# Cross-attention and gated feed-forward on one core: gather and splits ahead of masks and exponentials in step 7

## Chip, cores, metric

The kernel runs on one core of one Trainium2 chip. The metric is the device time of one execution in microseconds (us); lower is better. Engines are named as in the profile: PE is TensorE (PEld its weight loads), DVE is VectorE, ACT is ScalarE, POOL is GpSimd, SP is SyncE, which issues all transfers.

## What is computed

One transformer layer: cross-attention of 16 sequences of 128 tokens on 16 contexts of 128, then a gated feed-forward part, both with a residual. Cut to what matters:

```
x = x + xattn(layernorm(x), ctx)      # 32 heads of width 32, 8 groups of keys and values
x = x + (silu(h1) * h2) @ w3.T + b3   # h1, h2 = layernorm(x) @ w12.T + b12
# xattn: scores = q @ k.T / sqrt(32), masked; softmax; @ v; @ w_out.T
```

All arrays are float32. The kernel makes every product from pairs of float16: a value is split in a high and a low part, and a product is three matrix products (high by high, high by low, low by high).

## The kernel before, in words

The tokens come in 8 blocks of 256 (two sequences, `AB`). The attention part is a software pipeline of iterations t = 1 to 8, each of 8 steps s = 0 to 7. Iteration t does the attention of block t - 1, one group of 4 heads for 2 sequences per step (unit number g = 8 (t - 1) + s), and beside it the projections of block t (q in 8 units, k in 2, v in 2) and the output projection of block t - 2. The feed-forward part follows and is not touched here.

Each engine has its own instruction list, written out by hand in the same pair of loops, and waits on semaphores. What an engine does in a step is fixed; when, depends on the waits.

In step 7 (`LAST`) of iterations 2 to 6 the work is, by engine:

- **PE** (L1407 to L1485): the scores of group g (`scores`, L1464); the turning of one column, the largest absolute values of the next context block (`turn_top`, L1393, one row of 128 into a PSUM bank); the first half of v (`v_proj`, L1407); the turning of the first x tile of the block after next's projections, in two halves (`turn_x`, L1416, 4 + 4 instructions); the weighing of v with the probabilities of group g - 3 (`weigh`, L1485); the turning of the second x tile; the second half of v; and `spread_top` (L1400). Then step 0 of the next iteration: scores (L1464) and the first q unit (L1407), which begins only when all low parts of both x tiles have been written (`pe.wait_ge(s_dread, done("x", 2 * t + 1, 1))`).
- **DVE**: `mask_scores(g)` (L1889), eight instructions that scale and mask the scores and take each row's extreme; `gather_top` (L1687 to L1698), five small instructions that turn the gathered column into a power of two, the first of which frees its bank; `norm_prob(g, 0)` (L1905, L1908), which hands the inverse sums of the first sequence to POOL; the low part of v (`v_lo`, L1859) and of the first x tile (`x_lo`, L1854, two); the low part of the attention output of g - 3 (`attn_lo`, L1929); `norm_prob(g, 1)` (L1905, L1911); the two low parts of the second x tile; the low part of v's second half; `take_top` (L1710).
- **ACT**: `exps(g, 0)` (L1203, four exponentials with their sums), which waits for the first half of the masks; high part of v (L1193) and of the first x tile (L1166, two); high part of the attention output (L1173); `exps(g, 1)`; high parts of the second tile and of v's second half; high part of the probabilities (`prob_hi`, L1218).
- **POOL**: the low part of the probabilities of g - 1 (L975, two), and the normalising of the first sequence (L981).

A high part must be written by ACT before DVE takes the low part from the same PSUM bank; the low part frees the bank. Five banks go round (`banks()`), and the least recently taken is next. So in step 7 the first half of the second x tile goes into the bank of the gathered column, the second half into that of v, the second half of v into that of the first half of the first tile.

In iterations 3 to 6 DVE also looks at the weights of the feed-forward part for their maxima: in steps 2, 4 and 6 it reads 128 x 2048 values that SP has loaded into `look` (`max_of`, L1725; the load is L762). In step 6 this stands at the end of the step, behind `norm_prob(g, 1)` and `q_lo` (L1859). Iteration 6 has two more small instructions behind it, `in_pairs` (L1731, L1732), which join the maxima two by two.

Of the kernel before, what the change touches and what calls it, by code (L numbers as in the profile page):

```python
# [41 lines left out]
NB = TOK // AB  # L42
# [39 lines left out]
LAST = 7  # L82
# [68 lines left out]
def first_unit(t, s):  # L151

    if t < NB and s in FIRST_Q:
        return "q", t, FIRST_Q[s]
    if t >= 2 and s in FIRST_O:
        return "o", t - 2, FIRST_O[s]
    if t < NB and s == LAST:
        return "v", t, 0
    return projection(t, s) if t == 1 else None
# [8 lines left out]
def x_tiles(t, s):  # L168

    if t < NB - 1 and s == LAST:  # L170
        return 2 * t + 2, 2 * t + 3
    if t == NB - 1 and s in (3, LAST):
        return (2 * NB, 2 * NB + 1) if s == 3 else (2 * NB + 2, 2 * NB + 3)
    return None, None
# [133 lines left out]
def by_pool(g):  # L308

    return g in NORMED and g % GROUPS >= 3 and g < 56  # L310


def normed_count(g, kind=lambda n: n in NORMED):
# [33 lines left out]
def xattn_ffn(nc, x, ctx_t, mask, wq_t, wk_t, wv_t, wo_t, w12_t, b12_t, w3_t, b3_row, out):  # L347
# [8 lines left out]
    with ExitStack() as stack:  # L356
# [719 lines left out]
        def _(act):  # L1076
# [120 lines left out]
            def exps(g, u):  # L1197
                act.wait_ge(s_neg, U * g + u + 1)
                for j in range(HPG):
                    h = HPG * u + j  # L1200
                    head = e[:, g % 2, u, SEQ * j:SEQ * j + SEQ]
                    if g in NORMED:
                        ins = act.activation(head, head, ACT.Exp, bias=neg_max[:, g % 2, h:h + 1], scale=-1.0,  # L1203
                                             accum_out=p_sum[:, g % 2, u, j:j + 1])
                    else:
                        ins = act.activation(head, head, ACT.Exp, bias=neg_max[:, g % 2, h:h + 1], scale=-1.0)  # L1206
                ins.then_inc(s_exp, 1)
# [89 lines left out]
            def unit_hi(key):  # L1297
                if key and key[0] == "q":
                    q_hi(*key[1:])
                elif key and key[0] == "k":  # L1300
                    k_hi(*key[1:])
                elif key and key[0] == "v":
                    v_hi(*key[1:])

            for t in range(1, NB + 1):
                for s in range(STEPS):
                    g, (tile, tile2) = GROUPS * (t - 1) + s, x_tiles(t, s)
                    exps(g, 0)
                    if t == NB and s - 1 in H_AT:
                        hid_hi(0, H_AT[s - 1])  # L1310
                    if t == NB and s in H_AT:
                        exps(g, 1)
                        prob_hi(g)
                        silus(0, H_AT[s])
                        attn_hi(g - 3)
                        continue
                    unit_hi(first_unit(t, s))
                    if tile is not None:
                        x_hi(tile, 0)
                        x_hi(tile, 1)  # L1320
                    if g >= 3:
                        attn_hi(g - 3)
                    exps(g, 1)
                    if tile2 is not None:
                        x_hi(tile2, 0)
                        x_hi(tile2, 1)
                    unit_hi(second_unit(t, s))
                    if t < NB - 1 and s in (4, 6):
                        scale_rows(2 * t + s // 2)
                    prob_hi(g)  # L1330
                    if t == NB - 1 and s in (2, 6):
                        scale_rows(2 * NB + (s - 2) // 2)
                        scale_rows(2 * NB + (s - 2) // 2 + 1)
                    if t == 1 and s == 2:
                        o_high()
# [336 lines left out]
        def _(dve):  # L1672
# [396 lines left out]
            for t in range(1, NB + 1):  # L2069
                a = t - 1  # L2070
                block_scales(a)
                if t == 2:
                    link(dve.tensor_scalar(out_base[:, :], w_es[:, 0, col("o")], w_es[:, 0, col("kv", 1)], C_OUT,
                                           ALU.mult, ALU.mult))
                if t >= 2:
                    output_scales(t - 2)
                for s in range(STEPS):
                    g, name, (tile, tile2) = GROUPS * a + s, top_at(t, s), x_tiles(t, s)
                    if g >= 3:
                        divide(g - 3)  # L2080
                    mask_scores(g)
                    if t == NB and s - 1 in H_AT:
                        hid_lo(0, H_AT[s - 1])
                    if name:
                        gather_top(name)
                    if g >= 1 and g - 1 not in PLO_AWAY:
                        prob_lo(g - 1)
                    if g in NORMED:
                        norm_prob(g, 0)
                    if g in NORMED and t == NB and s in H_AT:  # L2090
                        norm_prob(g, 1)
                    unit_lo(first_unit(t, s))
                    if tile is not None:
                        x_lo(tile, 0)
                        x_lo(tile, 1)
                    if t == NB and s in H_AT:
                        first_half_read(0, H_AT[s])
                    if g >= 3:
                        attn_lo(g - 3)
                    if t < NB - 1 and s == 5:  # L2100
                        max_of(f"ctx{t + 1}", ctx_next, s_ctxload, 16 * t + 32)
                    if t == NB - 2 and s == 3:
                        max_of("b12", b12[:, :], s_b12, 16)
                    if (t, s) in O_LOW_AT:
                        o_low(O_LOW_AT.index((t, s)))
                    if t < NB - 1 and s in (2, 3):
                        row_stats(2 * t + s)
                    if t == NB - 1 and s in (1, 5):
                        row_stats(2 * NB + (s - 1) // 2)
                        row_stats(2 * NB + (s - 1) // 2 + 1)  # L2110
                    if t == NB - 1 and s == 4:
                        ffn_factors()
                    if g in NORMED and not (t == NB and s in H_AT):
                        norm_prob(g, 1)
                    if tile2 is not None:
                        x_lo(tile2, 0)
                        x_lo(tile2, 1)
                    unit_lo(second_unit(t, s))
                    if look_at(t, s):
                        max_of(look_at(t, s), look, s_look, look_count(look_at(t, s)))  # L2120
                    if look_at(t, s) == "w7":
                        in_pairs()
                    if t == NB and s in H_AT:
                        gate(0, H_AT[s])
                    if name:
                        take_top(name)
# [119 lines left out]
```

## Time and profile before

| | us |
|---|---|
| median of 3 runs (lowest to highest) | 1042.55 (1042.33 to 1042.89) |
| the profiled execution | 1045.69 |
| its span, first to last instruction | 1043.9 |
| PE busy | 1013.3 (97%) |
| DVE busy | 701.5 (67%) |
| ACT busy | 480.7 (46%) |
| POOL busy | 524.4 (50%) |

The span is shorter than the execution by what lies before the first and after the last instruction. Busy time says how long an engine had an instruction in hand; the ends of matrix products are modelled. A group that is called "DVE small L1687" is an instruction of DVE that writes the tile `small` on line 1687.

### The profile page before, as it was taken

What the parts mean: (1) busy time and instruction counts of PE and PEld (TensorE: products, weight loads), DVE (VectorE), ACT (ScalarE), POOL (GpSimd) and SP (SyncE); (2) the same over time, 40 slices, a digit from 0 to 9 for tenths busy, and PEclk for the clock granted to TensorE, in tenths of its full rate; (3) what the DMA queues carried; (4) which work ended last, traced back from release to release, by engine and by line L of the source; (5) the groups of instructions that cost most, each with busy time, mean ns of one, the idle gap of its engine ahead of it and who ended that gap; (6) DMA issues with size and microseconds to landing.
All of it is one profiled execution on the core that took longest, in us unless ns stands there. A gap on an engine that the chain in (4) does not pass through costs nothing.

```text
span 1043.9 us, 22125 instructions
## 1 busy us (share of the span) xinstructions
PE 1013.3 (97%) x8312; PEld 674.2 (65%) x8312; DVE 701.5 (67%) x2168; ACT 480.7 (46%) x1335; POOL 524.4 (50%) x500
## 2 busy tenths in 40 slices
PE   8897999999999999899999999999999999999998
PEld 7776867767677676676644444444444888468853
DVE  6789988878888788878769333746864446625431
ACT  5767666767666675664767310123431112211110
POOL 2869923746547375289967697148742301212000
PEclk8999999999999999999999999999999999999999
DMA  9559796998999989789854726494759641974301
GB/s 364 221 155 203 156 227 155 220 254 223 241 222 213 261 211 249 190 203 264 211 155 111 230 89 218 76 345 166 273 197 194 231 113 42 218 246 122 82 31 51
DMA packets 230779, 199.13 MB, mean 191 GB/s; under 512 B 177040, under 2 KB 187280, under 8 KB 225808
## 3 DMA queue, kind: packets, MB, share of 16 engines
q1 hardware_dynamic: 230672, 197.72, 70.5%
q8 instruction: 66, 1.08, 0.4%
q14 instruction: 41, 0.34, 0.1%
HBM read 119.04 MB, written 35.65 MB: 148 GB/s over the span
## 4 chain that ended last, share of the span: by engine, by line
PE 82%; DVE 8%; ACT 2%; issue 1%; DMA 1%; SPq 0%; DVEq 0%; ACTq 0%
PE bank_dense L1407 51%; PE bank_spare L1407 12%; PE bank_score L1563 6%; PE bank_spare L1563 6%; PE bank_av L1563 3%; DVE arena_attn L1889 3%; PE bank_score L1464 2%; DVE arena_in L1725 1%; PE bank_dense L1485 1%; DVE arena_attn L1899 1%; DMA k_scratch<-arena_in 1%; PE bank_spare L1485 1%; ACT arena_attn L1203 1%; PE bank_spare L1416 0%; ACT L1229 0%
## 5 line engine op out<-in xcount | busy, mean ns | idle before, releaser
L1407 PE MATMUL bank_dense<-arena_rows,arena_in 128*128 128x256 f16 (+1 forms) x1272 | 177.8, 298 | 1.6 <-POOL arena_in L913 1.0
L1407 PE MATMUL bank_dense<-arena_attn,arena_rows 128*128 128x512 f16 x768 | 166.4, 379 | 0.0
L975 POOL TENSOR_TENSOR arena_attn<-arena_attn 128x512 f16<-128x512 f32 x89 | 101.9, 1162 | 118.1 <-ACT arena_attn L1218 118.1
L1203 ACT ACTIVATE arena_attn<-arena_attn,arena_in 128x128 f32<-128x128 f32 x352 | 136.4, 391 | 47.8 <-DVE arena_in L1889 47.6
L1407 PEld LDWEIGHTS bank_dense<-arena_rows,arena_in 128*128 128x128 f16 x1272 | 123.0, 99 | 46.1 <-DVE arena_in L1737 1.3
L1889 DVE CUSTOM_DVE_ANT_0 arena_attn<-bank_score,arena_in 128x128 f32<-128x128 f32 x512 | 143.7, 346 | 1.6 <-PE bank_score L1464 1.1
L1407 PEld LDWEIGHTS bank_dense<-arena_attn,arena_rows 128*128 128x128 f16 x768 | 75.1, 98 | 90.2
L1407 PE MATMUL bank_dense<-arena_out,arena_attn 128*128 128x512 f16 x576 | 127.8, 379 | 0.0
L1407 PEld LDWEIGHTS bank_dense<-arena_out,arena_attn 128*128 128x128 f16 x576 | 55.5, 98 | 63.4
L1407 PE MATMUL bank_spare<-arena_rows,arena_in 128*128 128x256 f16 (+1 forms) x648 | 87.7, 293 | 0.0
L1407 PE MATMUL bank_dense<-arena_out,arena_in 128*128 128x512 f16 x384 | 83.0, 379 | 0.0
L1218 ACT ACTIVATE arena_attn<-arena_attn 128x1024 f16<-128x1024 f32 x64 | 67.3, 1052 | 27.9 <-DVE arena_attn L1911 27.7
L913 POOL TENSOR_TENSOR arena_in<-arena_in 128x512 f16<-128x512 f32 x62 | 75.5, 1217 | 5.0
L1995 DVE SCALAR_TENSOR_TENSOR arena_out<-bank_dense,small,arena_out 128x256 f32<-128x256 f32 x64 | 28.0, 478 | 74.1 <-PE bank_dense L1407 74.1
L1407 PEld LDWEIGHTS bank_spare<-arena_rows,arena_in 128*128 128x128 f16 x648 | 62.2, 98 | 19.9
L1407 PEld LDWEIGHTS bank_dense<-arena_out,arena_in 128*128 128x128 f16 x384 | 37.5, 98 | 45.4
L1203 ACT ACTIVATION_READ_ACCUMULATOR arena_attn<-arena_attn,arena_in 128x1 f32 x352 | 66.7, 189 | 0.0
L1206 ACT ACTIVATE arena_attn<-arena_attn,arena_in 128x128 f32<-128x128 f32 x160 | 50.9, 392 | 33.2 <-DVE arena_in L1889 33.2
L923 POOL TENSOR_TENSOR small<-small 128x1 f32<-128x1 f32 x32 | 20.3, 637 | 88.4 <-DVE small L1778 88.3
L1407 PE MATMUL bank_dense<-arena_in 128*128 128x256 f16 x456 | 54.0, 276 | 1.4 <-DVE arena_in L1744 1.4
L1051 POOL TENSOR_TENSOR arena_out<-arena_out,arena_rows 128x1024 f32<-128x1024 f32 x12 | 29.2, 2462 | 46.6 <-DMA arena_out<-x_scratch 46.6
L1407 PEld LDWEIGHTS bank_dense<-arena_in 128*128 128x128 f16 x456 | 44.2, 99 | 8.9 <-DVE arena_in L1744 1.7
(238 smaller groups left out, 1888.1 us busy)
## 6 DMA issues: line engine op xcount, KB each, us to landing
arena_rows<-x SPq DMA_DIRECT2D x32, 512.0 KB, 5.8
arena_in<-w_scratch SPq DMA_DIRECT2D x64, 256.0 KB, 3.0
arena_attn<-q_scratch SPq DMA_DIRECT2D x48, 256.0 KB, 4.4
arena_rows<-w_t SPq DMA_DIRECT2D x12, 1024.0 KB, 6.6
arena_rows<-ctx_t SPq DMA_DIRECT2D x8, 1024.0 KB, 6.0
q_scratch<-arena_attn SPq DMA_DIRECT2D x16, 512.0 KB, 5.2
x_scratch<-arena_rows SPq DMA_DIRECT2D x16, 512.0 KB, 3.9
arena_out<-x_scratch SPq DMA_DIRECT2D x16, 512.0 KB, 5.9
```

What stands on the lines that cost most here:

```text
L913: pool.tensor_tensor(lo, buf, hi, ALU.subtract).then_inc(ready, 1)
L975: ins = pool.tensor_tensor(p_split[:, g % 2, u, 1], e[:, g % 2, u], p_split[:, g % 2, u, 0], ALU.subtract)
L1051: ins = pool.tensor_tensor(y_res[:, u], y_res[:, u], b3_all, ALU.add)
L1203: ins = act.activation(head, head, ACT.Exp, bias=neg_max[:, g % 2, h:h + 1], scale=-1.0, accum_out=p_sum[:, g % 2, u, j:j + 1])
L1206: ins = act.activation(head, head, ACT.Exp, bias=neg_max[:, g % 2, h:h + 1], scale=-1.0)
L1218: act.activation(p_split[:, g % 2, :, 0], e[:, g % 2], ACT.Copy).then_inc(s_phi, 1)
L1407: ins = pe.matmul(dst, lhs(a, c), rhs(b, c), start=(c == chunks[0] and n == 0), stop=(c == chunks[-1] and n == 2))
L1464: ins = pe.matmul(B_SCORE[:, HALF * u + SEQ * j:HALF * u + SEQ * j + SEQ], q_stack[0:3 * DH, m // 4, j, m % 4, SEQ * u:SEQ * u + SEQ], k_s ...
L1485: ins = pe.matmul(dst[DH * j:DH * j + DH, SEQ * u:SEQ * u + SEQ], v[:, a % 2, u, m, 0:DH], prob_t[:, g % 2, u, piece, j], start=n == 0, st ...
L1563: ins = pe.matmul(seven(v, j), weights[:, a, P * c:P * c + P], rows[:, b, c], start=(c == 0 and n == 0), stop=(c == 3 and n == 2))
L1889: ins = dve.tensor_tensor_reduce(out=e[:, g % 2, h // HPG, SEQ * (h % HPG):SEQ * (h % HPG) + SEQ], in0=B_SCORE[:, SEQ * h:SEQ * h + SEQ], ...
L1995: ins = dve.scalar_tensor_tensor(out=cols, in0=bank("y", f, q)[:, 256 * k:256 * k + 256], scalar=c_ffn[:, 2 * h + k:2 * h + k + 1], in1=co ...
```

## The change

In step 7 of iterations 2 to 6 (`unit_first`) DVE does gather, the low part of v's first half and the two low parts of the first x tile ahead of the masks, and ACT does the high parts of the same ahead of the first exponentials. The maximum of step 6 moves up on DVE, ahead of `norm_prob(g, 1)`; `in_pairs` moves from the end of step 6 of iteration 6 to behind the masks of step 7. No instruction is added or taken away, and the lists of PE, POOL and SP stay as they are.

```diff
+def unit_first(t, s):
+
+    return s == LAST and 2 <= t < NB - 1
...
+                    if unit_first(t, s):
+                        unit_hi(first_unit(t, s))
+                        x_hi(tile, 0)
+                        x_hi(tile, 1)
                     exps(g, 0)
...
-                    unit_hi(first_unit(t, s))
-                    if tile is not None:
+                    if not unit_first(t, s):
+                        unit_hi(first_unit(t, s))
+                    if tile is not None and not unit_first(t, s):
                         x_hi(tile, 0)
                         x_hi(tile, 1)
...
+                    if unit_first(t, s):
+                        gather_top(name)
+                        unit_lo(first_unit(t, s))
+                        x_lo(tile, 0)
+                        x_lo(tile, 1)
                     mask_scores(g)
+                    if t == NB - 2 and s == LAST:
+                        in_pairs()
                     if t == NB and s - 1 in H_AT:
                         hid_lo(0, H_AT[s - 1])
-                    if name:
+                    if name and not unit_first(t, s):
                         gather_top(name)
...
-                    unit_lo(first_unit(t, s))
-                    if tile is not None:
+                    if not unit_first(t, s):
+                        unit_lo(first_unit(t, s))
+                    if tile is not None and not unit_first(t, s):
                         x_lo(tile, 0)
                         x_lo(tile, 1)
...
+                    if look_at(t, s) and s == 6:
+                        max_of(look_at(t, s), look, s_look, look_count(look_at(t, s)))
                     if g in NORMED and not (t == NB and s in H_AT):
                         norm_prob(g, 1)
...
-                    if look_at(t, s):
+                    if look_at(t, s) and s < 6:
                         max_of(look_at(t, s), look, s_look, look_count(look_at(t, s)))
-                    if look_at(t, s) == "w7":
-                        in_pairs()
```

On ACT, steps 6 and 7 of iteration 5, before. `v_high` is the high part of v, arena_rows with a bank as its source the high part of an x tile, `x4` the four exponentials of one sequence, 128x256 from a bank the high part of q or of the attention output:

```order
L1180 ACTIVATE arena_attn<-bank_dense 128x256
L1218 ACTIVATE arena_attn<-arena_attn 128x2x512
L1203 ACTIVATE arena_attn<-arena_attn,arena_in 128x128 x4
L1193 ACTIVATE v_high<-bank_spare 128x8x32
L1166 ACTIVATE arena_rows<-bank_dense 128x4x128 x2
L1173 ACTIVATE arena_attn<-bank_dense 128x256
```

The same place of the changed kernel, whose lines are numbered 5 higher here:

```order
L1185 ACTIVATE arena_attn<-bank_dense 128x256
L1223 ACTIVATE arena_attn<-arena_attn 128x2x512
L1198 ACTIVATE v_high<-bank_spare 128x8x32
L1171 ACTIVATE arena_rows<-bank_dense 128x4x128 x2
L1208 ACTIVATE arena_attn<-arena_attn,arena_in 128x128 x4
L1178 ACTIVATE arena_attn<-bank_dense 128x256
```

The four exponentials have moved behind the high parts of v and of the first x tile.

On DVE, end of step 6 of iteration 5 and step 7, before. `ISA` with `bank_score` is a mask instruction, of which there are eight and one stands here; TENSOR_REDUCE of arena_rows is the weight maximum:

```order
L1929 SCALAR_TENSOR_TENSOR arena_attn<-bank_dense,arena_attn 128x256
L1911 SCALAR_TENSOR_TENSOR arena_attn<-arena_attn,bank_av 128x512
L1725 TENSOR_REDUCE arena_in<-arena_rows 128x1
L1889 ISA arena_attn,arena_in<-bank_score,arena_in 128x128
L1687 TENSOR_REDUCE small<-bank_spare 1x1
L1698 TENSOR_TENSOR small<-small 1x2
L1908 TENSOR_SCALAR arena_attn<-bank_av 128x4
L1859 SCALAR_TENSOR_TENSOR v_low<-bank_spare,v_high 128x256
L1854 TENSOR_TENSOR arena_rows<-bank_dense,arena_rows 128x4x128 x2
```

The same of the changed kernel, whose lines are numbered 10 higher here:

```order
L1939 SCALAR_TENSOR_TENSOR arena_attn<-bank_dense,arena_attn 128x256
L1735 TENSOR_REDUCE arena_in<-arena_rows 128x1
L1921 SCALAR_TENSOR_TENSOR arena_attn<-arena_attn,bank_av 128x512
L1697 TENSOR_REDUCE small<-bank_spare 1x1
L1708 TENSOR_TENSOR small<-small 1x2
L1869 SCALAR_TENSOR_TENSOR v_low<-bank_spare,v_high 128x256
L1864 TENSOR_TENSOR arena_rows<-bank_dense,arena_rows 128x4x128 x2
L1899 ISA arena_attn,arena_in<-bank_score,arena_in 128x128
L1918 TENSOR_SCALAR arena_attn<-bank_av 128x4
```

The masks have moved behind gather, v split and x splits, and the maximum ahead of the normalising of step 6.

## Rows read from the trace of the kernel before

**Rows 1.** Waits of PE, iterations 2 to 6: total us, times, longest.

```profile
PE bank_spare L1416 <- DVE small L1687: 3.2, 3, 1.1
PE bank_dense L1416 <- DVE small L1687: 2.9, 1, 2.9
PE bank_spare L1416 <- DVE v_low L1859: 2.3, 4, 0.6
PE bank_dense L1416 <- DVE v_low L1859: 0.6, 1, 0.6
```

**Rows 2.** Timeline, PE, step 7 of iteration 5: start, us, instruction, [idle].

```profile
363.62 2.78 PE L1407 MATMUL bank_spare<-arena_in 128*128 128x256 f16 x24
366.24 1.04 PE L1416 MATMUL bank_dense<-arena_in,arena_rows 128*128 128x128 f32 x8
...
370.66 2.79 PE L1407 MATMUL bank_dense<-arena_in 128*128 128x256 f16 x24
...
374.29 2.79 PE L1407 MATMUL bank_dense<-arena_rows,arena_in 128*128 128x256 f16 x24
```

**Rows 3.** Timeline, DVE, the same stretch.

```profile
364.02 2.28 DVE L1725 TENSOR_REDUCE arena_in<-arena_rows 128x1 f32<-128x2048 f32 x1
366.21 0.34 DVE L1889 CUSTOM_DVE_ANT_0 arena_attn<-bank_score,arena_in 128x128 f32<-128x128 f32 x1
...
369.92 1.28 DVE L1854 TENSOR_TENSOR arena_rows<-bank_dense,arena_rows 128x512 f16<-128x512 f32 x2
...
372.12 0.19 DVE L1905 RECIPROCAL bank_av<-arena_attn 128x4 f32<-128x4 f32 x1 [0.60 <-ACT arena_attn L1203]
...
372.95 1.28 DVE L1854 TENSOR_TENSOR arena_rows<-bank_spare,arena_rows 128x512 f16<-128x512 f32 x2
```

**Rows 4.** Timeline, ACT, the same stretch.

```profile
367.41 0.40 ACT L1203 ACTIVATE arena_attn<-arena_attn,arena_in 128x128 f32<-128x128 f32 x1 [1.69 <-DVE arena_in L1889]
...
368.97 0.36 ACT L1193 ACTIVATE v_high<-bank_spare 128x256 f16<-128x256 f32 x1
369.23 1.06 ACT L1166 ACTIVATE arena_rows<-bank_dense 128x512 f16<-128x512 f32 x2
370.18 0.38 ACT L1173 ACTIVATE arena_attn<-bank_dense 128x256 f16<-128x256 f32 x1
370.45 0.40 ACT L1203 ACTIVATE arena_attn<-arena_attn,arena_in 128x128 f32<-128x128 f32 x1
...
373.49 0.39 ACT L1193 ACTIVATE v_high<-bank_dense 128x256 f16<-128x256 f32 x1 [0.43 <-PE bank_dense L1407]
```

**Rows 5.** Timeline, PE, iteration 2: v's first half, next iteration's first projection.

```profile
170.81 2.78 PE L1407 MATMUL bank_spare<-arena_in 128*128 128x256 f16 x24
...
180.04 2.79 PE L1407 MATMUL bank_dense<-arena_rows,arena_in 128*128 128x256 f16 x24
```

**Rows 6.** Timeline, PE, the same two of iteration 6.

```profile
428.90 2.78 PE L1407 MATMUL bank_dense<-arena_in 128*128 128x256 f16 x24
...
442.77 2.78 PE L1407 MATMUL bank_dense<-arena_rows,arena_in 128*128 128x256 f16 x24
```

**Rows 7.** Timeline, DVE, the pairing of maxima in iteration 6.

```profile
431.60 0.64 DVE L1731 TENSOR_TENSOR arena_in<-arena_in 128x4 f32<-128x4 f32 x1
432.28 1.09 DVE L1732 COPY arena_in<-arena_in 128x4 f32<-128x4 f32 x1
```

**Rows 8.** Windows: stretch, us, PE busy (instructions), granted clock, DMA share, GB/s.

```profile
95.00:97.80 2.80, 0.00 (x0) 1.00 0.84 196
436.90:440.40 3.50, 3.27 (x16) 0.51 0.89 290
```

**Rows 9.** Timeline, POOL and DVE, iteration 2.

```profile
172.98 2.28 POOL L975 TENSOR_TENSOR arena_attn<-arena_attn 128x512 f16<-128x512 f32 x2 [4.95 <-ACT arena_attn L1218]
174.21 1.06 DVE L1698 TENSOR_TENSOR small<-small 1x2 f32<-1x2 f32 x1
```

**Rows 10.** Loads of `look` by SP (L762): us from issue to landing.

```profile
DMA to landing us min/median/max: 5.6/6.6/8.7
```

## The prediction

> **What bounds the kernel now.** The first view is the page: TensorE (PE) is busy 97% of the span, so only what keeps PE waiting, or slows it, can move the time. The second is the list of waits of PE over iterations 2 to 6 [rows 1]: all of its waits of any size there stand in front of line 1416, the turning of the next x tiles in step 7, 9.0 us together (3.2 + 2.9 + 2.3 + 0.6). Four times the releaser is the first instruction of the gather (small, L1687), which frees the PSUM bank that the gathered column stood in; five times it is the low split of v, which frees v's bank. By iteration that is 1.1 + 0.6 in 3, 4 and 5, 2.9 + 0.6 in 6, and for iteration 2 what is left of the v waits, 2.3 less three times 0.6, about 0.45.
>
> The third view is the timeline of one such step, iteration 5 [rows 2 to 4]. DVE takes the weight maximum (2.28), then the eight mask instructions from 366.21, then gather and v split, and the x splits from 369.92. PE had v ready at 366.4, stands 1.1 and 0.6 us on the way, and comes to v's second half at 370.66 only. The reader should look one step further, at what PE waits for next: the first projection of the next iteration, at 374.29, starts as soon as the low splits of the **second** x tile are done (two instructions from 372.95, 1.34 us before PE starts). In code: q of unit 0 waits for `done("x", 2t+1, 1)`. So in step 7 there are two chains that end at nearly one time: the banks, and masks, exponentials, normalising, splits of the second tile. The change shortens the first and lengthens the second.
>
> **The second chain, part by part** (iteration 5, all [rows 3, 4]). From the start M of the masks: first exponentials at M + 1.20 (366.21 to 367.41). They take 1.56 (v's high part starts at 368.97), v's and the first tile's high parts 1.21 (to 370.18), the attention copy 0.27, and the second exponentials start at 370.45, that is M + 4.24. Normalising comes 1.67 later (372.12), the second tile's low splits 0.83 later (372.95), PE's projection 1.34 later (374.29). Sum M + 8.08 today.
>
> *Exponentials.* The change takes v's and the first tile's high parts out from between the two exponential groups. That is 1.21 less; the attention copy stays. The chain behind the masks becomes M + 6.87.
>
> *Masks.* They now wait behind gather, v split and first-tile x splits. The gather no longer matters: its column is ready before v. What sets M is PE: v starts at V = 363.62, the eight turns end at 366.24 + 1.04 = 367.28, that is V + 3.66. An ACT operation starts 0.04 after PE's end (v's second half: PE ends 373.45, ACT starts 373.49) [rows 2, 4]; a high part of x takes about 0.59 and a hand-over of 0.04 follows; a low split holds DVE about 0.60, an estimate from 1.28 for two, whose end overlaps with the instruction behind [rows 3, 4]. The last turned half thus gives M = V + 3.66 + 0.04 + 0.04 + 0.59 + 0.04 + 0.60 = V + 4.97 = 368.59, the second 0.04 because ACT is just then through with the half before. Today M is V + 2.59. **The masks start 2.38 us later and the chain behind them is 1.21 us shorter: the next iteration starts 1.17 us later**, at V + 11.84 against V + 10.67. PE no longer waits before the turns, and waits about 2.9 us after the scores instead. Iterations 3 and 4 show the same rows as 5, so 3 x 1.17 = 3.51.
>
> *Iteration 2* has no weight maximum, its masks start early and PE begins the next block at V + 9.23 (170.81 to 180.04) [rows 5]. With the same V + 11.84 it loses 2.61.
>
> *Iteration 6* has the pairing of maxima as well, and PE begins the next block at V + 13.87 (428.90 to 442.77) [rows 6]. At V + 11.84 it gains 2.03. The pairing (0.64 + 1.09, [rows 7]) moves behind the masks: they end at M + 2.2, the pairing at worst at M + 3.9, the first normalising and the low attention split by M + 4.65; the second normalising waits for exponentials until M + 4.70. So it costs nothing, by 0.05 us.
>
> *The maximum of step 6* moves ahead of the second normalising. It is hidden if its weights are there: DMA takes 5.6 to 8.7 us to land, 6.6 in the middle [rows 10], from an issue some 6 us ahead of the new place. In the middle case normalising, and ACT's high probabilities behind it, are done just before v is; 8.7 would cost some 1.5 us in one iteration. I take 0, upper bound +1.5. Sum of the chain: 2.61 + 3.51 - 2.03 = **+4.1 us**.
>
> *The clock.* PE stood still for the whole of 95.00 to 97.80, and after it, and after iteration 6's stalls of 2.87 and 0.62, the granted clock fell to its lower level of 1.2 GHz (0.51 over 436.90 to 440.40) [rows 8]; after the pairs of 1.1 and 0.6 it did not. The fall costs about half of that stretch of 3.5 us, 1.6 to 1.75, say 1.6. The last one is part of iteration 6's 13.87 and goes with its stall. The new stall of 2.9 us in one piece stands nearer to the ones that were followed by a fall. It comes five times; the bounds are no fall (0) and five (+8). I take three: +4.8.
>
> **Where a page speaks.** At 174.21 the last gather instruction took 1.06 us and ended with a GpSimd operation that began at 172.98 and ran 2.28 [rows 9]. The Trainium skill, page "SBUF — State Buffer", section "Who interferes with whom", says that a VectorE instruction with two SBUF inputs and a GpSimd instruction that reads SBUF exclude each other, the later one waiting in full. By that rule, which the row agrees with, the gather of iterations 3 to 6, now beside GpSimd's probability subtraction, may end up to 1.0 us later, and the masks 0.26 later, four times: 1.0 more in the sum. By the rows alone it is 0, since most gathers were short. The same rule makes the moved pairing cheaper, which changes nothing.
>
> **The sum.** The profiled execution took 1045.69 (span 1043.9), the median of the runs is 1042.55; the shift is the same for both. 1042.55 + 4.1 + 4.8 = **1051.4 us**.
>
> **The rivals.**
> 1. *Chain as computed, clock stays up* (none or one fall). For it: the stall is one piece of 2.9, shorter than the sum of either that was followed by a fall. 1042.55 + 4.1 + 0 to 1.6 = 1046.7 to 1048.3. Chance 0.33.
> 2. *All five stalls drop the clock*: 1054.7. Chance 0.08.
> 3. *Faster: the second chain does not hold the next iteration.* The stalls of 9.0 and the one fall of 1.6 go and nothing comes: 1032. For it speaks iteration 2, where PE begins the next block 1.4 us sooner after v than in 5, so the chain can be shorter when it starts early. Against it, that the maximum of 2.28 ahead of the masks is replaced by a wait for PE's turns and ACT, and the rows of iteration 5 show no slack at all. It decides at the mask's start: were it 0.8 us earlier than V + 4.97 in every iteration (4.1 / 5), the sum would be 0. Part of it would give 1036 to 1040. Chance 0.08.
> 4. *Nothing to see* (within 0.2%): M is mis-sized by that 0.8 and the clock stays up: about 1042.5. Chance 0.05.
> That the change doesn't do what it says is out, as the order of instructions shows the moved rows; PE's own order is the same.
>
> **How the numbers follow.** Forecast, two to four falls of the clock: 0.46, 1049.9 to 1053.1, in the middle 1051.4. A measurement of this kernel can tell about 0.2%, 2.1 us, from no change. Slower by more: 0.46 + 0.33 + 0.08 = 0.87; same 0.05; faster 0.08. The range takes the forecast, rival 1 and most of rival 2: 1045.0 to 1055.0, which leaves out rivals 3 and 4 and the upper edge.
>
> **What would show it.** Right: no wait of PE at the turns of x in iterations 2 to 6, and five new waits of 2.5 to 3.5 us before the first projection of iterations 3 to 7, released by a low split of x; masks starting 5.0 us after v's start; distance from v's start to the next iteration's first projection 11.8 in all five; granted clock at its lower level after two to four of them. Wrong: that distance near 9 or 10, or masks at V + 4.2 or before. A distance above 12.5 would mean that the weight maximum or the gather is late.

## The result, and the profile after

| | before | after |
|---|---|---|
| median of 4 runs, us (lowest to highest) | 1042.72 (1042.33 to 1043.22) | 1058.08 (1056.06 to 1060.31) |
| the profiled execution, us | 1045.69 | 1056.06 |
| its span, us | 1043.9 | 1054.3 |
| granted clock of PE in it | 0.993 | 0.990 |
| PE busy, us (share) | 1013.3 (97%) | 1014.1 (96%) |
| DVE busy, us (share) | 701.5 (67%) | 708.8 (67%) |

The changed kernel is slower: after over before is 1.0141, 95% interval 1.0128 to 1.0154, 14.7 us by this ratio and 15.4 by the medians. The two profiled executions differ by 10.4 only, because that of before lies 3.0 above its median and that of after 2.0 below (the lowest of its runs): 10.4 + 3.0 + 2.0 = 15.4.

The one large wait of PE in iterations 2 to 6, which answers to [rows 1] (total, times, longest):

```profile
PE bank_dense L1417 <- DVE arena_rows L1864: 16.4, 5, 3.6
```

All nine waits at the turns of x are gone, 9.0 us. Five others have come, 16.4 us, one in each iteration, in front of the first projection (L1417) and released by a low split of x (L1864). Iteration 5 in the timeline of PE, beside [rows 2]; the last row's bracket is the idle time in front of it:

```profile
371.02 2.78 PE L1417 MATMUL bank_spare<-arena_in 128*128 128x256 f16 x24
373.64 1.04 PE L1426 MATMUL bank_dense<-arena_in,arena_rows 128*128 128x128 f32 x8
...
375.06 1.09 PE L1426 MATMUL bank_spare<-arena_in,arena_rows 128*128 128x128 f32 x8
375.99 2.78 PE L1417 MATMUL bank_dense<-arena_in 128*128 128x256 f16 x24
...
379.01 0.62 PE L1474 MATMUL bank_score<-arena_attn 96*128 96x128 f16 x8
382.96 4.24 PE L1417 MATMUL bank_dense<-arena_rows,arena_in 128*128 128x256 f16 x22 [3.33 <-DVE arena_rows L1864]
```

DVE in the same stretch, beside [rows 3]:

```profile
368.93 2.29 DVE L1735 TENSOR_REDUCE arena_in<-arena_rows 128x1 f32<-128x2048 f32 x1
...
373.12 0.15 DVE L1708 TENSOR_TENSOR small<-small 1x2 f32<-1x2 f32 x1
...
374.91 1.29 DVE L1864 TENSOR_TENSOR arena_rows<-bank_dense,arena_rows 128x512 f16<-128x512 f32 x2 [0.16 <-ACT arena_rows L1171]
376.12 0.34 DVE L1899 CUSTOM_DVE_ANT_0 arena_attn<-bank_score,arena_in 128x128 f32<-128x128 f32 x1
...
380.80 0.19 DVE L1915 RECIPROCAL bank_av<-arena_attn 128x4 f32<-128x4 f32 x1 [1.09 <-ACT arena_attn L1208]
...
381.63 1.28 DVE L1864 TENSOR_TENSOR arena_rows<-bank_spare,arena_rows 128x512 f16<-128x512 f32 x2
```

And ACT, beside [rows 4]:

```profile
374.28 1.09 ACT L1171 ACTIVATE arena_rows<-bank_dense 128x512 f16<-128x512 f32 x2
377.31 0.40 ACT L1208 ACTIVATE arena_attn<-arena_attn,arena_in 128x128 f32<-128x128 f32 x1 [1.95 <-DVE arena_in L1899]
```

Read it from v's start V = 371.02. The x splits end and the masks start at 376.12, V + 5.10. The exponentials follow 1.19 later, the second normalising at 380.80, the low splits of the second tile at 381.63, the projection at 382.96, V + 11.94. ACT stood still for 1.95 us and DVE twice for about a microsecond (1.05 before the low part of v, and 1.09), while PE had run out of work at 379.63.

The clock, in the five stretches from the scores before a stall to the scores behind it (stretch, us, PE busy, granted clock, DMA share, GB/s), beside [rows 8]:

```profile
176.20:188.50 12.30, 8.97 (x82) 0.72 0.52 155
244.80:254.60 9.80, 6.46 (x82) 1.00 0.70 215
311.20:322.70 11.50, 7.92 (x81) 0.85 0.66 187
379.00:390.40 11.40, 8.07 (x81) 0.85 0.60 156
447.20:459.00 11.80, 8.73 (x84) 0.86 0.44 124
```

After four of the five stalls part of the work ran at 1.2 GHz in place of 2.4; this is called a fall of the clock from here on. After the second, of 3.34 us where the first had 3.33, there was none.

**A table that the experiments are read by.** The scores of every step start at a row of their own (L1464 before), so the distance between two such rows is the length of a step. Given is step 7 of iteration t plus step 0 of iteration t + 1, in us, worked out from these rows; "filled" is an experiment below, in which PE has work in the stall and no fall of the clock is seen.

| t | before | after | filled |
|---|---|---|---|
| 2 | 9.34 + 6.25 = 15.59 | 8.56 + 12.26 = 20.82 | 8.55 + 9.75 = 18.30 |
| 3 | 10.62 + 6.41 = 17.03 | 8.55 + 9.76 = 18.31 | 8.55 + 9.75 = 18.30 |
| 4 | 10.62 + 6.42 = 17.04 | 8.55 + 11.52 = 20.07 | 8.55 + 9.76 = 18.31 |
| 5 | 10.63 + 6.40 = 17.03 | 8.55 + 11.43 = 19.98 | 8.55 + 9.75 = 18.30 |
| 6 | 13.86 + 6.78 = 20.64 | 8.55 + 11.85 = 20.40 | 8.55 + 10.70 = 19.25 |

After minus before is 5.23 + 1.28 + 3.03 + 2.95 - 0.24 = 12.2. Step 7 itself became 2.1 shorter in iterations 3 to 5, where its waits at the turns went, and step 0 behind it 3.4 to 5.1 longer. Iteration 3, where the clock stayed up, shows the bare price of the longer chain: 1.28. In iteration 4, 0.25 of the 3.03 is a weight maximum that came late (V + 12.19 to the projection in place of 11.94), not the clock.

### The profile page after: what moved, and what is told of

It is laid out like the page before. It is cut to its first block, busy times and chain, and to the rows that moved or that the text cites. A ratio compares the mean times of both kernels' runs of the same rounds, so it can differ in the third digit from the quotient of the medians.

```text
span 1054.3 us, 22125 instructions
## 1 busy us (share of the span) xinstructions
PE 1014.1 (96%) x8312; PEld 674.3 (64%) x8312; DVE 708.8 (67%) x2168; ACT 480.8 (46%) x1335; POOL 524.6 (50%) x500
## 4 chain that ended last, share of the span: by engine, by line
PE 78%; DVE 9%; ACT 5%; issue 2%; DMA 1%; POOL 1%; SPq 0%; DVEq 0%; ACTq 0%
PE bank_dense L1417 48%; PE bank_spare L1417 11%; PE bank_score L1573 6%; PE bank_spare L1573 5%; DVE arena_attn L1899 3%; PE bank_av L1573 3%; ACT arena_attn L1208 2%; PE bank_score L1474 2%; DVE arena_attn L1909 1%; DVE arena_rows L1864 1%; PE bank_dense L1495 1%; POOL arena_attn L980 1%; DMA k_scratch<-arena_in 1%; DVE arena_attn L1921 1%; ACT arena_rows L1299 1%
## 5 line engine op out<-in xcount | busy, mean ns | idle before, releaser
L1417 PE MATMUL bank_dense<-arena_rows,arena_in 128*128 128x256 f16 (+1 forms) x1272 | 182.9, 303 | 18.3 <-DVE arena_rows L1864 16.4
L1417 PEld LDWEIGHTS bank_dense<-arena_rows,arena_in 128*128 128x128 f16 x1272 | 125.3, 101 | 65.7 <-DVE arena_rows L1864 17.3
L1417 PE MATMUL bank_dense<-arena_attn,arena_rows 128*128 128x512 f16 x768 | 166.4, 379 | 0.0
L1417 PEld LDWEIGHTS bank_dense<-arena_attn,arena_rows 128*128 128x128 f16 x768 | 75.1, 98 | 90.2
L1417 PE MATMUL bank_dense<-arena_out,arena_attn 128*128 128x512 f16 x576 | 127.8, 379 | 0.2 <-DVE arena_attn L1939 0.2
L1417 PEld LDWEIGHTS bank_dense<-arena_out,arena_attn 128*128 128x128 f16 x576 | 55.5, 98 | 63.7 <-DVE arena_attn L1939 0.4
L1417 PE MATMUL bank_spare<-arena_rows,arena_in 128*128 128x256 f16 (+1 forms) x648 | 87.8, 292 | 0.0
L1417 PE MATMUL bank_dense<-arena_out,arena_in 128*128 128x512 f16 x384 | 83.0, 379 | 0.0
L1417 PEld LDWEIGHTS bank_spare<-arena_rows,arena_in 128*128 128x128 f16 x648 | 62.2, 98 | 19.9
L1417 PEld LDWEIGHTS bank_dense<-arena_out,arena_in 128*128 128x128 f16 x384 | 37.6, 98 | 45.3
L1417 PE MATMUL bank_dense<-arena_in 128*128 128x256 f16 x456 | 52.8, 273 | 1.4 <-DVE arena_in L1754 1.4
L1417 PEld LDWEIGHTS bank_dense<-arena_in 128*128 128x128 f16 x456 | 43.9, 98 | 7.5 <-DVE arena_in L1754 1.7
```

The source lines that it names most:

```text
L1417: ins = pe.matmul(dst, lhs(a, c), rhs(b, c), start=(c == chunks[0] and n == 0), stop=(c == chunks[-1] and n == 2))
```

## The experiments

Each ratio is to runs of the kernel before on the same chip. Line numbers in the rows of an experiment are a few higher than in the changed kernel, where its edit adds lines.

### All splits ahead of the masks

If the splits of the second tile hold the next iteration because they stand behind masks and exponentials, they can be put ahead as well:

```diff
                         x_hi(tile, 1)
+                        attn_hi(g - 3)
+                        x_hi(tile2, 0)
+                        x_hi(tile2, 1)
                     exps(g, 0)
...
                         x_lo(tile, 1)
+                        attn_lo(g - 3)
+                        x_lo(tile2, 0)
+                        x_lo(tile2, 1)
                     mask_scores(g)
...
```

(the same calls are left out where they stood before)

> The changed kernel, with the attention output's split and the second x tile's four splits also ahead of the masks and exponentials. Theory (the next iteration waits for the second tile's splits, which stand behind the masks): the first projection starts 9.1 to 9.6 us after v in all five iterations, PE's long stalls go, clock 0.993: 1035 us (1033 to 1039). Rival (something else holds the next iteration, such as masks or scores): the stall stays at 3 us and comes in front of the scores, 1054 or more. In between, if masks that start 1.4 us later still are the next bound: about 1043.

Measured: 1044.65 against 1043.30, ratio 1.0008 (0.9999 to 1.0018), no difference from the kernel before. Waits of PE, iterations 2 to 6 (total, times, longest):

```profile
PE bank_score L1477 <- DVE arena_in L1902: 5.0, 5, 1.2
PE bank_dense L1420 <- DVE arena_attn L1942: 4.8, 4, 1.3
```

The first projection starts 9.45 to 9.69 us after v, much as forecast; the stalls before it are gone, and with them the falls of the clock behind them (1.00 in the windows around all five, 0.993 to 0.998 over whole runs). So the second tile's splits were what held the next iteration. But two waits took their place. The scores wait about 1.0 for the masks, which now stand behind all splits: steps 7 and 0 take 9.58 + 6.24 = 15.82 in iteration 3, 1.21 less than before. Three steps later the output projection (L1420) waits 1.17 to 1.32 for `attn_lo` (L1942), and step 3 takes 10.15 in place of 8.81. The 1.2 gained is given back as 1.34. Over all iterations of this trace steps 7 and 0 gave 6.5, 3.3 of it in iteration 6, and later steps took it back. The forecast of 1035 failed. The scores' wait had been named as the case in between (about 1043), which is where the time came out; the wait three steps later I had not looked for: DVE's list is late by what the masks were late, and it has not caught up three steps on.

### Part two alone

```diff
 def unit_first(t, s):
 
-    return s == LAST and 2 <= t < NB - 1
+    return False
```

> Only the second part of the change: the weight maximum of step 6 ahead of the normalising, the pairing behind the masks; gather and splits stay behind the masks as before. Theory: masks start 1.3 us after v instead of 2.6, so the first projection comes at 9.3 us after v instead of 10.7 in iterations 3 to 5 and instead of 13.9 in 6: 4.0 + 4.5 = 8.5 less, 1034 us (1033 to 1037). Rival (this part is what costs, since normalising and high probabilities come later): above 1043.

Measured: 1038.09 against 1043.30, ratio 0.9950 (0.9933 to 0.9966). Moving the maximum and the pairing alone makes the kernel 5.2 us **faster**. Steps 7 and 0 take 15.59 in iterations 3 and 5 (before 17.03), and 17.03 in iteration 6 (before 20.64). In iteration 4 they take 17.25, no gain. There the maximum waited for its weights, as this row of DVE shows:

```profile
294.26 2.29 DVE L1735 TENSOR_REDUCE arena_in<-arena_rows 128x1 f32<-128x2048 f32 x1 [1.68 <-DMA arena_rows<-w_t]
```

With that landing PE waited at the turns again, 1.29 + 0.66. The forecast of 1034 (1033 to 1037) was missed by 4.1 us. Iteration 4 is 1.6 of it (1.4 forecast as gained, 0.2 lost). Another 0.9 is iteration 6, 3.6 gained in place of 4.5: PE still stood there for 0.70 + 0.63, though the clock stayed at 1.00, where it had fallen before. And 0.8 is that the kernel before took 1043.30 in these runs, not 1042.55.

### Part one in iteration 2 only

```diff
-    return s == LAST and 2 <= t < NB - 1
+    return s == LAST and t == 2
```

(maximum and pairing where they were before)

> The kernel before with the new order of step 7 in iteration 2 alone, maxima as before. Theory: chain +2.6 us, and the clock falls after the one stall, for one or two stretches: +1.7 to +3.4, together 1047 to 1049. If the clock does not fall after a single stall: 1045.3. Rival (chain not as computed): no change, 1042.7.

Measured: 1050.14 against 1043.30, ratio 1.0060 (1.0041 to 1.0080), a little above the 1047 to 1049 that were expected. One stall of 3.33 us stands in the trace. Two windows, around it and around iteration 3's two waits of before, 1.07 and 0.62:

```profile
176.60:187.80 11.20, 7.88 (x80) 0.85 0.54 166
235.60:247.70 12.10, 10.40 (x101) 0.86 0.78 213
```

The clock fell after both. In the trace of before the same two waits of iteration 3 were followed by none. So the falls are not tied to one length of a stall: the same place of the program has one in the trace of this kernel and none in that of the kernel before.

### The same, with PE kept busy

Eighteen turnings of the identity matrix into the bank that the projection then overwrites, between the scores and the wait. They add work and change no result:

```diff
+                dst = begin("q", t, m)
+                if m == 0 and t == 3:
+                    for _ in range(18):
+                        pe.transpose(dst[:, 0:P], ident[:, :], ident[:, :])
                 if m == 0:
                     pe.wait_ge(s_dread, done("x", 2 * t + 1, 1))
-                dst = begin("q", t, m)
...
```

> The same 18 turns with the new order in iteration 2 alone (the one run before, which took 1050.1 against 1043.3). Theory: only the chain of 2.6 us is left, 1045.9 (1045 to 1047). Rival (what made that run 6.8 slower instead of 2.6 is not the clock): 1049 or more.

Measured: 1046.28 against 1043.87, ratio 1.0020 (1.0010 to 1.0031). As expected. The chain of iteration 2 alone: steps 7 and 0 take 8.56 + 9.76 = 18.32, 2.73 more than before, with the clock up:

```profile
175.80:185.50 9.70, 8.55 (x101) 1.00 0.63 193
```

Between this kernel and the one above lies only the filling: 0.0060 less 0.0020, that is 0.0040 or 4.2 us, with intervals that are wide beside it (0.002 to either side for the first, 0.001 for the second), and still more than one fall of 1.6. In the two traces it is two falls, the second behind iteration 3's old waits, which the filled kernel doesn't show.

### All five stalls filled

The same with `3 <= t <= 7`, on top of the whole change:

> The changed kernel with 18 turns of the identity matrix on TensorE (about 2.4 us) ahead of the first projection of iterations 3 to 7, into the bank that this projection then overwrites; nobody reads them. They stand in the stall of 2.8 to 3.6 us. Theory (a late chain of +4.1 us, and the rest is the lower clock after the stalls): 1047 us (1045.5 to 1048.5), granted clock 0.995 or more, the first projection still 11.8 to 12.0 us after v. Rival (the clock is only a sign, and a transfer or another engine is late behind the stall): 1054 or more, because the turns bring nothing forward.

Measured: 1054.40 against 1043.87, ratio 1.0099 (1.0081 to 1.0117). This missed by 7 us, and the time is the rival's. Half as many turnings went with it:

> The changed kernel with 9 turns (about 1.2 us) instead of 18, so that 1.7 to 2.4 us of each stall stay idle. Half the dose. Clock theory: between the changed kernel and the filled one; if what counts is how much of the stall is idle, most falls go: 1047 to 1050. Rival (the turns help by something else than activity, such as their place in the queue): no difference to the run with 18.

Measured: 1055.43, ratio 1.0104 (1.0084 to 1.0125). This too is above its range. The trace of the half filled kernel shows a fault of the filling that both have. In iteration 7 the projection has another bank, freed late, and the filling stood behind that wait (L1445), so the stall was not filled but made longer:

```profile
PE bank_dense L1417 <- DVE arena_rows L1867: 8.0, 4, 2.0
PE bank_dense L1445 <- DVE arena_rows L1867: 2.2, 1, 2.2
```

Its windows around the five stalls, which are 2.00 us of standing still in the first four and 2.24 in the last:

```profile
177.30:186.90 9.60, 7.47 (x89) 1.00 0.62 195
243.70:255.00 11.30, 9.17 (x90) 0.85 0.66 197
311.30:321.00 9.70, 7.57 (x90) 1.00 0.77 193
377.80:389.10 11.30, 9.18 (x89) 0.85 0.52 166
446.00:458.10 12.10, 9.63 (x92) 0.86 0.41 119
```

Four stalls of one length, two with a fall and two without. So 2.00 us of standing still, in place of 3.33, did not keep the clock up.

The fault mended: in iteration 7 the turnings stand ahead of the column `w_in`, in its bank, which is free.

```diff
+                if name == "w_in":
+                    for _ in range(18):
+                        pe.transpose(dst[:, 0:P], ident[:, :], ident[:, :])
                 pe.transpose(dst[0:k, 0:P], w_max[:, at:at + k], ident[:, :]).then_inc(ready, 1)
...
-                if m == 0 and 3 <= t <= 7:
+                if m == 0 and 3 <= t <= 6:
```

> The changed kernel with the 18 turns again, now inside the stall in iteration 7 too: in the run before them they stood there behind a bank that comes free only at the end of the stall, so that they lengthened it by 2.2 us instead of filling it. In iterations 3 to 6 they stand as before. Theory (chain of +4.8 us by the step lengths, the rest is the lower clock): 1048.5 us (1047 to 1050) beside 1043.9 of the kernel before, clock 0.994 or more. Rival (a cost of 5 us or more besides both): 1053 or more.

Measured: 1052.69 against 1044.02, ratio 1.0086 (1.0073 to 1.0099). This is 4 us above the forecast and just below the rival's 1053, so chain and clock alone do not make up the time. The clock is up in all five windows; two of them, and the stall of iteration 5 filled:

```profile
178.10:187.70 9.60, 8.46 (x98) 1.00 0.64 195
...
444.80:455.30 10.50, 8.97 (x101) 1.00 0.53 120
```

```profile
377.18 0.62 PE L1480 MATMUL bank_score<-arena_attn 96*128 96x128 f16 x8
377.92 2.18 PE L1448 MATMUL bank_dense<-arena_in 128*128 128x128 f32 x18
381.12 2.79 PE L1420 MATMUL bank_dense<-arena_rows,arena_in 128*128 128x256 f16 x24 [1.02 <-DVE arena_rows L1870]
```

Two things follow. First, the falls cost 1.0141 less 1.0086, that is 0.0055 of 1043, **5.7 us** (1.9 to either side by the two intervals), and the change is still 8.7 us slower without them (9.0 by the ratio). Second, the table's last column gives the chain without falls: 2.71 + 1.27 + 1.27 + 1.27 - 1.39 = **5.1 us**, not 8.7. Part of what is left is in step 3, where PE waits for `attn_lo` in each of iterations 3 to 6. The row of PE, and DVE's row of `attn_lo` (L1945):

```profile
399.42 0.61 PE L1480 MATMUL bank_score<-arena_attn 96*128 96x128 f16 x8
400.24 0.60 PE L1420 MATMUL bank_dense<-arena_out,arena_attn 128*128 128x512 f16 x2 [0.21 <-DVE arena_attn L1945]
```

```profile
399.77 0.41 DVE L1945 SCALAR_TENSOR_TENSOR arena_attn<-bank_spare,arena_attn 128x256 f16<-128x256 f32 x1
```

Before, it stood so, with that step's scores at 392.59:

```profile
391.50 0.41 DVE L1929 SCALAR_TENSOR_TENSOR arena_attn<-bank_spare,arena_attn 128x256 f16<-128x256 f32 x1
```

`attn_lo` started 1.09 ahead of the scores and now starts 0.35 behind them. Step 3 takes 9.19 in place of 8.81 in iterations 3 to 6, 4 x 0.38 = 1.5, and step 4 of iteration 6 takes 9.92 in place of 9.32, where the turning of a column waits 0.44 for a maximum. Together **2.1 us**. This is the same lateness as in the first experiment, smaller. In the half filled kernel it shows as a pattern: step 3 takes 9.18 and 9.20 in the two iterations whose stall had no fall before it, and 8.80 and 8.81 in the two where the clock fell and PE was late as well. The sum so far is 7.2 of 8.7. Another 0.7 comes in the trace behind iteration 6. The last 0.8 I can't place, since it is the difference between a trace and the medians.

### Part one alone

```diff
                     mask_scores(g)
-                    if t == NB - 2 and s == LAST:
-                        in_pairs()
...
-                    if look_at(t, s) and s == 6:
-                        max_of(look_at(t, s), look, s_look, look_count(look_at(t, s)))
```

(both where they were before)

> Only the first part of the change: gather, v and first-tile splits ahead of masks and exponentials; the maximum of step 6 and the pairing stay at the end of step 6. Theory: the maximum ends 2.7 us after v's start, gather and v split follow, masks 0.2 us later than in the changed kernel in iterations 3 to 5 and 1.9 later in 6: 1058 + 2.5 = 1060.5 us (1059 to 1064). So the second part would give little on top of the first, though alone it gives 5. Rival (the parts add up: second part -5 here too): 1063 or more.

Measured: 1061.49 against 1044.02, ratio 1.0169 (1.0156 to 1.0182). The time is in the range; its parts are not. The masks start at V + 5.92 in iterations 3 to 5 and V + 6.83 in 6, which is 0.6 to 0.8 later than in the changed kernel in the first three, not 0.2, and 1.7 later in 6. Five stalls of PE stand in the same place, 2.84 to 3.66 each. Two of the windows around them, iterations 2 and 3:

```profile
176.70:188.80 12.10, 8.78 (x80) 0.72 0.48 155
245.70:257.30 11.60, 7.94 (x80) 0.85 0.48 164
```

Here the clock fell after all five. So the parts are +17.5 for part one and -5.2 for part two, and together +15.4, not +12.3: once the masks wait for PE's turns, an early maximum buys little.

### Two tries for a better kernel

From part two alone, with every weight maximum moved up, those of steps 2 and 4 too:

```diff
-                    if look_at(t, s) and s == 6:
+                    if look_at(t, s):
...
```

> The maximum moved ahead of the normalising in steps 2 and 4 too, gather and splits as before. In the run with step 6 alone moved (1038.1), iteration 4 still stood 1.3 us before the turns because its weights landed late, behind a load that waits for the maximum of step 4. Theory: that load goes out 1 to 2 us earlier, iteration 4 becomes like 3 and 5: 1036.5 (1035 to 1038). Rival (steps 2 and 4 have no slack for it, and normalising or splits make TensorE wait there): 1040 or more.

Measured: 1042.07 against 1043.87, ratio 0.9986 (0.9967 to 1.0004), which is worse than part two alone. I expected the buffer `look` to come free sooner and its load to land sooner; in part two alone the weights of iteration 4 were there at 294.3, and here at 294.4. The earlier maxima now stand in front of their own loads: DVE waits for weights seven times, 13.2 us in total, against once, 1.7 us, in part two alone. The longest is in iteration 5:

```profile
343.97 2.29 DVE L1735 TENSOR_REDUCE arena_in<-arena_rows 128x1 f32<-128x2048 f32 x1 [3.90 <-DMA arena_rows<-w_t]
```

In step 7 of that iteration PE stood longer than before, and the clock fell, one row and one window:

```profile
365.89 0.30 PE L1426 MATMUL bank_spare<-arena_in,arena_rows 128*128 128x128 f32 x1 [1.84 <-DVE small L1697]
```

```profile
359.90:372.00 12.10, 9.90 (x97) 0.86 0.82 212
```

The other: part two alone, with the gather between the two halves of the masks, so that the exponentials of the first sequence don't wait for it.

```diff
...
+                    if h == HPG - 1 and between:
+                        gather_top(between)
...
```

> The second part of the change alone (1038.1 before), with the gather between the two halves of the masks. It frees the gathered column's bank 1.1 us earlier and delays only the second half of the masks, by 0.85, which the second exponentials wait for by 0.05 at most. Theory: the stall before the second tile of 0.7 in iteration 6 goes, iteration 4 (1.3) is held by the masks' chain anyway: 1037.3 us (1035.5 to 1039). Rival (the second half of the masks is on the path, as exponentials and scores wait for it): 1040 or more.

Measured: 1037.31 against 1044.02, ratio 0.9949 (0.9936 to 0.9962), as expected. Iteration 6 takes 9.58 + 6.78 in place of 10.25 + 6.78, the others the same within 0.4. It can't be told from part two alone by the intervals. Both beat the kernel before by 0.5%; they are the kernels to keep.

## Why the prediction was right in sign and too small

Forecast 1051.4 in a range of 1045.0 to 1055.0; the median is 1058.08, outside. The sign and the two chains were right. The step that failed is the term for the clock: three falls at 1.6, +4.8, where the profiled run shows four that cost 6.9, and the other runs, at a lower clock still, lie 1.8 to 4.3 us above it. Beside it the chain was 1.0 too short, and a term had been put at nothing without a reason: what DVE's lateness does behind the next projection, 2.1 us when the clock stays up. By the steps of the prediction:

- **Two chains, one shortened and one lengthened: right.** The waits at the turns went, five new ones came where they were said to come, released by what was named. Rival 3, that the second chain would not hold the next iteration, is refuted by the run with all splits ahead.
- **Masks at V + 4.97: 5.10** in iterations 2, 3, 5 and 6 (5.34 in 4). **The chain behind them 6.87: 6.84.** **The distance 11.84: 11.94** in iterations 2, 3 and 5, 11.95 in 6, 12.19 in 4.
- **Sum of the chain +4.1: 5.1** (filled run). Iteration 2 was 2.61 and measured 2.71; iterations 3 to 5 were 1.17 and measured 1.27 each. Most of the difference is iteration 6, -1.39 in place of -2.03, of which 0.38 is a wait behind the projection, for the last instruction of the gather in iteration 7, that the distance to the first projection doesn't contain.
- **The new stall "about 2.9": 3.33** in iterations 2, 3 and 5, 3.58 in 4, 2.85 in 6. I had added the two old waits and the 1.17. But step 7 without them became 2.07 shorter, not 1.69: stops of PE at the turns cost more than the list of waits says. Part two alone shows it too: one stop of 0.45 at the turns, and 9.34 in place of 8.55. The new stall took all that step 7 lost, and the longer chain besides: 2.07 + 1.27 = 3.34. The early stall of the kernel before, which the prediction compared this one with, is 2.8 as the window of [rows 8] has it, but PE was idle for 3.30 us there.
- **The clock +4.8: this term failed.** Three falls at 1.6 were taken. The profiled run has four, and they cost, by after less filled in the table, 2.5 + 0 + 1.8 + 1.7 + 1.1 = 7.1 us, less 0.25 in iteration 4 for the late maximum: 6.9. The one in iteration 2 was followed by a lower clock for about twice as long (0.72 over 12.3 us), which the cap of five times 1.6 left out. The other runs had a lower clock still (0.982 to 0.986, against 0.990). The prediction took three falls with no more than the two of before to go by, and its middle was a guess between none and five.
- **A term was missing: DVE's lateness handed on to step 3.** I followed the chain to the next iteration's first projection and stopped there. Without falls it costs 2.1 us more. With them it is mostly hidden, since PE is then late as well: after shows it once, 9.20 in step 3 of iteration 4. That fits the falls' costing 6.9 by the steps but 5.7 by the ratios: removing them brings back 1.7 of the hidden waits, though the interval around 5.7 would allow no difference as well.
- **The maximum of step 6, 0: right** in iterations 3, 5 and 6. In iteration 4 its weights landed late, and normalising, high probabilities, the high part of v and the masks behind them came 0.24 later; that is 0.25 of the bound of +1.5:

```profile
302.39 2.29 DVE L1735 TENSOR_REDUCE arena_in<-arena_rows 128x1 f32<-128x2048 f32 x1 [1.39 <-DMA arena_rows<-w_t]
```

- **The pairing, 0: right.** Behind the masks it took

```profile
446.49 0.17 DVE L1741 TENSOR_TENSOR arena_in<-arena_in 128x4 f32<-128x4 f32 x1
446.69 0.17 DVE L1742 COPY arena_in<-arena_in 128x4 f32<-128x4 f32 x1
```

  0.34 together, against 1.73 in [rows 7].
- **1.0 more by DVE and POOL in each other's way: did not come.** The gather's last instruction took 0.15 in all five iterations. In iteration 5 it began at 373.12, and POOL's subtraction at 373.20, as the high probabilities were ready only then; in no iteration did the two overlap by more than 0.1. The Trainium skill's rule (page "SBUF — State Buffer", section "Who interferes with whom") is not refuted by this: there was hardly an overlap for it to act on, and the pairing, 1.73 before and 0.34 now, moved as the prediction read it there (its second instruction, a copy with one source, is not what the sentence on two inputs speaks of). The error was in where POOL stood.

The account of the profiled pair closes: from step 7 of iteration 2 to step 0 of iteration 7, 5.1 for the chain, 6.9 for falls, 0.25 for late weights and 0.4 for the handed-on wait, 12.6 before rounding. Ahead of it the trace of before had lost 2.5 more than that of after, 2.1 of it before the first scores, which start at 62.10 against 59.99 (granted clock up to 60 us: 0.94 against 0.97). It was not the stall near 95 us [rows 8], which both have. And 0.3 comes behind: 12.6 - 2.5 + 0.3 = 10.4, the difference of the spans. The other 5.0 lie between these two executions and their medians. That the clock is lower in the slower runs of after is seen; which stalls it followed is open, since they have no trace.

## What to carry to other kernels

When a wait is removed by moving work ahead of other work, follow the work that was passed over to everything that waits for it, also steps later: here masks held the exponentials, these the splits, these the next projection, and DVE's lateness came out once more three steps on. Ask also in how many pieces PE will stand still: waits of 1.1 + 0.6 became one of 3.3, and the clock cost about as much again as the chain (5.7 to 6.9 against 5.1). And try the parts of a change apart: one of these two alone was worth 5 us, the other cost 17.

## What the hardware showed that was not expected

- Whether the clock falls after a stall of a given length is not fixed. Stalls of 2.00 us were followed by a fall in two of four cases, one of 3.33 by a low stretch about twice as long as the others and the next, of 3.34, by none; 1.07 + 0.62 by none in the trace of before and by one (0.86 over 12.1 us) in another kernel at the same place. The early stall of the kernel before, 3.30 us, was followed by a fall (0.50 over 99.80 to 101.00); the same stall in the changed kernel was longer, and the clock stayed at 1.00 behind it:

```profile
94.89 0.19 PE L1503 MATMUL bank_av<-v_high,arena_attn 128*128 128x33 f16 x1 [3.45 <-DMA arena_attn<-arena_attn]
```

- Turnings of a float32 identity matrix, which are no work for the result, kept the clock up: 18 of them, 2.18 us, cut 3.33 us of standing still to 1.02 or less, and the clock stayed at 1.00 in all six windows of the two traces. Nine, with 2.00 left, did so in two of four.
- Stops of PE in front of the turnings lengthen the step by more than their idle time: 2.07 for two stops of 1.69 together, 0.79 for one of 0.45. The step lengths are measured from start to start. Whether the idle time is listed too short, as the ends of the turnings are modelled, or the turnings themselves are slower behind a stop was not tried.
